# Feed-forward's first rows and weight pieces prepared in the second attention's last batch

## The reference, cut to what matters

```python
x = x + tanh(g_xattn[0]) * L0_xattn(layernorm(x), ctx)
x = x + tanh(g_ffn[0])   * L0_experts(layernorm(x))
x = x + tanh(g_xattn[1]) * L1_xattn(layernorm(x), ctx)     # "second attention", 16 heads of 32, 256 + 16 keys
x = x + tanh(g_ffn[1])   * L1_ffn(layernorm(x))

def L1_ffn(x):                                             # 512 -> 2048 -> 512
    h = gelu(x @ proj1.T + proj1_bias)                     # exact gelu
    return h @ proj2.T + proj2_bias
```

## Time and profile before

| | us |
|---|---|
| median of three runs | 3754.83 |
| lowest and highest | 3752.32, 3757.24 |
| the profiled execution | 3753.35 |
| its span on the core | 3751.6 |
| TensorE busy | 3583.4 (96%) |
| VectorE busy | 2179.9 (58%) |
| ScalarE busy | 1822.8 (49%) |
| GpSimd busy | 1532.9 (41%) |
| attention, first instruction to first of the feed-forward | 2243.5 to 2988.9 |
| feed-forward | 2988.9 to 3751.6 |

### The profile page before, as it was taken

How to read it: one execution, slowest core, us unless ns; L and a number is a source line. 1 busy time by engine, 2 the same in 40 slices (tenths; PEclk the granted TensorE clock), 3 DMA queues, 4 the chain that set the end, 5 groups by cost and what they waited for, 6 DMA issues and landing times. The chain is left out here.

```text
span 3751.6 us, 68000 instructions
## 1 busy us (share of the span) xinstructions
PE 3583.4 (96%) x23268; PEld 3105.6 (83%) x23268; DVE 2179.9 (58%) x5409; ACT 1822.8 (49%) x4696; POOL 1532.9 (41%) x1536
## 2 busy tenths in 40 slices
PE   7999999999999997799999987999999699999999
PEld 7999999999999996799999975666666478877887
DVE  6666666556666665567666776777777352222221
ACT  4444454544444443455555535777777442222222
POOL 3333333534444444456655645666776330000000
PEclk9999999999999998899999998999999799999999
DMA  4566665315666651666666652222121120000000
GB/s 151 178 222 228 229 217 210 125 67 213 220 216 220 220 207 57 241 236 237 238 229 235 237 183 79 60 65 65 61 69 36 55 79 23 23 23 23 23 23 23
DMA packets 228534, 520.22 MB, mean 139 GB/s; under 512 B 12289, under 2 KB 29058, under 8 KB 224242
## 3 DMA queue, kind: packets, MB, share of 16 engines
q1 hardware_dynamic: 123634, 296.43, 22.8%
q10 hardware_dynamic: 94432, 187.71, 13.6%
q0 software_dynamic: 10272, 33.63, 2.7%
HBM read 266.58 MB, written 251.13 MB: 138 GB/s over the span
## 5 line engine op out<-in xcount | busy, mean ns | idle before, releaser
L672 POOL TENSOR_SCALAR a_prob<-a_prob,a_rinv 128x256 f32<-128x256 f32 x512 | 471.3, 932 | 835.9 <-DVE a_rinv L855 835.9
L619 ACT ACTIVATE a_prob<-a_prob,a_low_bias 128x256 f32<-128x256 f32 x512 | 256.5, 502 | 458.7 <-DVE a_low_bias L846 458.7
L2209 DVE TENSOR_TENSOR f_h_lo<-f_h_f,f_h_hi 128x512 fp32r<-128x512 f32 x128 | 104.0, 813 | 456.4 <-ACT f_h_hi L2166 456.4
L1122 PE MATMUL e_gb<-e_xt_hi,in_hi 128*128 128x256 f32 x1248 | 355.0, 284 | 5.7 <-DVE e_xt_lo L1248 5.7
L1123 PE MATMUL e_gb<-e_xt_lo,in_hi 128*128 128x256 f32 x1248 | 354.8, 284 | 0.0
L1124 PE MATMUL e_gb<-e_xt_hi,in_lo 128*128 128x256 f32 x1248 | 354.7, 284 | 0.0
L1106 POOL TENSOR_TENSOR e_act_hi<-e_act_f,e_zeros 128x256 fp32r<-128x256 f32 x156 | 235.2, 1508 | 285.2 <-DVE e_act_f L1268 273.6
L2164 ACT ACTIVATE f_h_f<-f_hb,f_b_sb 128x512 f32<-128x512 f32 x128 | 88.0, 688 | 477.3 <-PE f_hb L2090 417.8
L422 PE MATMUL a_pj<-a_xt,a_wq_hi 128*128 128x256 f32 x1024 | 310.2, 303 | 0.9 <-DVE a_q_lo L705 0.9
L424 PE MATMUL a_pj<-a_xt,a_wq_lo 128*128 128x256 f32 x1024 | 289.4, 283 | 0.0
L423 PE MATMUL a_pj<-a_xt,a_wq_hi 128*128 128x256 f32 x1024 | 289.1, 282 | 0.0
(11 more groups left out here) (311 smaller groups left out, 11463.7 us busy)
## 6 DMA issues: line engine op xcount, KB each, us to landing
w_raw<-in_w_gate SPq DMA_DIRECT2D x39, 2048.0 KB, 7.9
x_sorted<-a_blank ACTq DMA_DIRECT2D x42, 1792.0 KB, 6.5
y_sorted<-a_blank ACTq DMA_DIRECT2D x42, 1792.0 KB, 8.7
w_raw<-in_w_out SPq DMA_DIRECT2D x39, 1024.0 KB, 5.0
e_xg<-x_sorted SPq DMA_DIRECT2D x39, 512.0 KB, 8.5
y_sorted<-e_y_sb SPq DMA_DIRECT2D x39, 512.0 KB, 2.8
xt_rows<-a_xt SPq DMA_DIRECT2D x16, 1024.0 KB, 5.1
a_xt<-xt_rows SPq DMA_DIRECT2D x16, 1024.0 KB, 6.2
```

The source lines that it names most:

```text
L619: e = nc.scalar.activation(prob[:, u % 4, t], prob[:, u % 4, t], ACT.Exp, bias=low_bias[:, u % 2, t:t + 1], scale=-1.0, accum_out=rsum[:, ...
L672: p = nc.gpsimd.tensor_scalar(prob[:, u % 4, t], prob[:, u % 4, t], rinv[:, u % 2, t:t + 1], None, ALU.mult)
L1122: nc.tensor.matmul(out, a_hi, b_hi, start=start, stop=False)
```

## The change

Part of what `first` did is moved into the last steps of the attention, and the results are left in buffers that live on:

- `w_raw` becomes `raw_in` and `raw_out`. `raw_in`, `in_hi`, `in_lo`, `dca_hi`, `dca_lo`, the identity, b1 and the feed-forward's gate are kept over both stages; `raw_out` ends with the attention. The class `Ahead` names the places: the first rows and the normalised rows in the two halves of `nrm`, pieces 0 and 1 in the places of the attention's `wd` and `wkv`, the transposed rows' high and low part in the place of `wq`. Piece 2 goes over `wo` later.
- SP, behind all loads of the attention: piece 0 into `y_sb`, rows 0 to 511 into `raw_in`, piece 1 into `x2`; b1 and the gate among the constants at the attention's start.
- In the last batch, counted in steps from the last pair (`past`): ACT casts half a piece at the end of steps -9, -8, -5, -4, and two transposed column blocks at the end of steps 0 and 1. DVE makes low parts in steps -8, -7, -4, -3, statistics in -6 and -5, the normalised rows in -2, low parts of the transposed rows in 1 and 2. POOL has the root in -4. PE transposes 8 blocks in step 0 and 8 in step 1, into the score banks; the low and high parts then come from there. Groups 0 and 1 of `last_out` move from step 2 to step 0.
- The feed-forward begins with `hidden(0, 0, 0)`. SP loads piece 2, piece 3, rows 512 to 1023, b2. DVE multiplies b2 by the gate behind the low part of step 1 and adds it to the first rows in step 12. All low parts from piece 2 on are GpSimd's, as before.

```diff
+class Ahead:
+    def __init__(self, b1, gate, first, b1_sb, gate_t, raw_in, in_hi, in_lo):
+        self.x_first, self.xn = raw_in[:, 1, :, 0:D], raw_in[:, 1, :, D:2 * D]
+        self.first_hi, self.first_lo = ([w[:, 1, n:n + 2].rearrange("p a (b d) -> p (a b) d", b=2) for n in (2, 0)] for w in (in_hi, in_lo))
+        self.xt_hi, self.xt_lo = in_hi[:, 0, :, 0:D], in_lo[:, 0, :, 0:D]
...
 # attention, sync
+            sp.wait_ge(y_used, B)
+            sp.dma_start(ff_raw[0], ahead.first[0]).then_inc(ff_loaded[0], 16)
+            sp.wait_ge(ready["qk"], GROUPS * (B - 1))
+            for bb in range(2):
+                sp.wait_ge(x_stored[bb], 64)
+            sp.dma_start(ahead.x_first, x_out[0:2 * S, :].rearrange("(t p) d -> p t d", p=P)).then_inc(ff_x_loaded, 16)
+            sp.wait_ge(x_used, B)
+            sp.dma_start(ff_raw[1], ahead.first[1]).then_inc(ff_loaded[1], 16)
 # attention, tensor
+            def turn_ahead(m):
+                pe.wait_ge(ff_xn, 1)
+                pe.wait_ge(e_done, B * PAIRS + m + 1)
+                for j in range(2):
+                    c = 2 * m + j
+                    for t in range(4):
+                        mm = nc.tensor.transpose(sc[:, m, j, t * P:(t + 1) * P], ahead.xn[:, t, c * P:(c + 1) * P], ident[:])
+                    mm.then_inc(ff_turned, 1)
...
+                if past == 0:
+                    turn_ahead(0)
                 if pair(i, u - 2):
                     turn_p(i, u - 2, 0)
+                if past == 0:
+                    last_out(i, (u - 2) // PAIRS, "o0", [0, 1])
+                if past == 1:
+                    turn_ahead(1)
                 if past == 2:
-                    last_out(i, u // PAIRS - 1, "o0", list(range(GROUPS - 1)))
+                    last_out(i, u // PAIRS - 1, "o0", [2])
...
+                if past == 0:
+                    last_out(i, (u - 2) // PAIRS, "o1", [0, 1])
                 if past == 2:
-                    last_out(i, u // PAIRS - 1, "o1", list(range(GROUPS - 1)))
+                    last_out(i, u // PAIRS - 1, "o1", [2])
 # attention, scalar
+            def split_ahead(n, half):
+                rows = slice(2 * half, 2 * half + 2)
+                act.wait_ge(ff_loaded[n], 16)
+                act.wait_ge(ready["v0"], B)
+                nc.scalar.copy(ahead.first_hi[n][:, rows], ff_raw[n][:, rows]).then_inc(ff_hid, 1)
...
+                past = LOOP * i + u - (B * PAIRS - 1)
+                if past in (-9, -8):
+                    split_ahead(0, past + 9)
+                if past in (-5, -4):
+                    split_ahead(1, past + 5)
+                if past in (0, 1):
+                    for c in range(2 * past, 2 * past + 2):
+                        turned_ahead(c)
 # attention, vector
+                if past in (-8, -7):
+                    low_ahead(0, past + 8)
+                if past in (-6, -5):
+                    normalize_ahead(past + 6)
+                if past in (-4, -3):
+                    low_ahead(1, past + 4)
+                if past == -2:
+                    normalize_ahead(2)
+                if past in (1, 2):
+                    for c in range(2 * past - 2, 2 * past):
+                        turned_low_ahead(c)
 # feed_forward
-            load_rows(0, 0)
-            load(0)
-            sp.dma_start(ident[:], identity).then_inc(id_loaded, 16)
-            load(1)
...
+            load(2)
             load(3)
             load_rows(1, 1)
-            sp.wait_ge(t_ready, FC)
-            load(2)
+            sp.dma_start(b2_sb[:], b2).then_inc(b_loaded, 16)
...
-            def first():
-                for c in range(FC):
-                    turn(0, c)
-                low_done(pe, 0)
-                hidden(0, 0, 0)
+            hidden(0, 0, 0)
```

More of the change, by code:

```diff
@@ L1904, in take, with low_ahead, normalize_ahead, turned_low_ahead @@
                 op.then_inc(taken[use], 1)
+            def low_ahead(n, half):
+                rows = slice(2 * half, 2 * half + 2)
+                dve.wait_ge(ff_hid, 2 * n + half + 1)
+                low(ahead.first_lo[n][:, rows], ff_raw[n][:, rows], ahead.first_hi[n][:, rows]).then_inc(ff_lod, 1)
+            def normalize_ahead(part):
+                x = ahead.x_first
+                if part == 0:
+                    dve.wait_ge(ff_x_loaded, 16)
+                    for t in range(4):
+                        l = V.bn_stats(ff_stats[:, t], x[:, t])
+                    l.then_inc(ff_stat, 1)
+                elif part == 1:
+                    dve.wait_ge(ff_stat, 1)
+                    dve.nop(nofuse=True)
+                    for t in range(4):
+                        l = V.bn_aggr(ff_mv[:, t], ff_stats[:, t])
+                    l.then_inc(ff_stat, 1)
+                    dve.wait_ge(ff_stat, 2)
+                    V.tensor_scalar(ff_var[:], ff_mv[:, :, 1], LN_EPS, None, ALU.add).then_inc(ff_stat, 1)
+                else:
+                    dve.wait_ge(ff_root, 1)
+                    dve.wait_ge(ready["qk"], GROUPS * B)
+                    for t in range(4):
+                        l = V.tensor_scalar(ahead.xn[:, t], x[:, t], ff_mv[:, t, 0:1], ff_rstd[:, t:t + 1], ALU.subtract, ALU.mult)
+                    l.then_inc(ff_xn, 1)
+            def turned_low_ahead(c):
+                dve.wait_ge(ff_xt_hid, c + 1)
+                low(ahead.xt_lo[:, c], sc[:, c // 2, c % 2], ahead.xt_hi[:, c]).then_inc(ff_lod, 1)
             def step(i, u):
@@ L2041, in feed_forward, with all_chunks @@
         LINKS = 4
-        def all_chunks(eng, first, chunk):
-            first()
+        def all_chunks(eng, chunk):
             for b in range(2):
@@ L2137, in chunk @@
                         turn(n + 1, TURN[j])
-            all_chunks(pe, first, chunk)
+            all_chunks(pe, chunk)
         @block.scalar
@@ L2143, in split @@
             def split(n):
-                act.wait_ge(w_loaded[n % 4], 16 * (n // 4 + 1))
-                nc.scalar.copy(pieces[n][1], raw(n)).then_inc(w_hid, 1)
+                act.wait_ge(w_loaded[n % 4], 16 * ((n - 2) // 4 + 1))
+                nc.scalar.copy(w_hi[n], raw(n)).then_inc(w_hid, 1)
             def turned(n, b, c):
-                act.wait_ge(t_ready, FC * n + c + 1)
-                nc.scalar.copy(xt_hi[:, b, c], tb[c % 2][:]).then_inc(xt_hid, 1)
-            def first():
-                split(0)
-                act.wait_ge(c_loaded, 16 * len(consts))
-                nc.scalar.activation(gate_t[:], gate_t[:], ACT.Tanh).then_inc(gate_done, 1)
-                split(1)
-                for c in range(FC):
-                    turned(0, 0, c)
+                act.wait_ge(t_ready, FC * (n - 1) + c + 1)
+                nc.scalar.copy(xt_hi[b][:, c], tb[c % 2][:]).then_inc(xt_hid, 1)
             def chunk(i, b, last, is_first=False):
@@ L2198, in chunk @@
                 if is_first:
-                    for n in range(4, len(pieces)):
+                    for n in range(4, PIECES):
                         split(n)
-            all_chunks(pool, lambda: root(0), chunk)
+            all_chunks(pool, chunk)
         @block.vector
@@ L2246, in turned, with first_bias, first_sum @@
             def turned(n, b, c):
[L2247 to L2263 removed]
+                dve.wait_ge(xt_hid, FC * (n - 1) + c + 1)
+                low(xt_lo[b][:, c], tb[c % 2][:], xt_hi[b][:, c]).then_inc(xt_lod, 1)
+            def first_bias():
+                dve.wait_ge(b_loaded, 16)
+                V.tensor_scalar(b2_sb[:], b2_sb[:], gate_t, None, ALU.mult).then_inc(bias_done, 1)
+            def first_sum():
                 dve.wait_ge(bias_done, 1)
[L2265 removed]
+                for t in range(TC):
+                    l = V.tensor_tensor(x_sb[0][:, t], x_sb[0][:, t], b2_sb[:], ALU.add)
+                l.then_inc(bias_done, 1)
             def chunk(i, b, last, is_first=False):
```

184 lines of the change are left out of this document (92 added, 92 removed).

## The result

| | before | after |
|---|---|---|
| median, us | 3754.83 | 3731.69 |
| lowest and highest | 3751.82, 3757.24 | 3726.12, 3734.68 |
| profiled execution, us | 3753.35 | 3731.69 |
| its span | 3751.6 | 3729.9 |
| TensorE busy | 3583.4 | 3581.6 |

The ratio of after to before is 0.9939, 95% interval 0.9924 to 0.9953. The medians differ by 23.1 us, the two profiled executions by 21.7. So the traces have 21.7 us to explain, against a forecast sum of 20.3.

What follows compares the result with a forecast made beforehand. The prediction took TensorE to bound the feed-forward, idle before it behind a 20 us latency chain. Terms -20.5 + 0 + 0.8 + 0 + 1.2 - 1.8 = -20.3 from 3753.35, plus 1.5, gave 3734.6 us; range 3727.5 to 3742.

Steps and rivals of the forecast that it cites:

- The feed-forward's start: TensorE's first feed-forward matmul starts 0.3 us after the stage opens, at 2989.2 in place of 3009.7: -20.5 us.
- Piece 2 and the pieces behind it: Weight loads at the feed-forward's start keep up with the earlier first matmul: 0, at most +2 us.
- the row of the same position: Piece 2, now the stage's first load, lands in 5.7 us like the load formerly in that place, so nothing waits: 0.
- The clock at the feed-forward's start: First feed-forward matmuls run at half speed for about 4.6 us, 1.5 us more than before: +0.8 us, range -0.5 to +0.8.
- The bias step: VectorE's b2 times gate, between low parts 1 and 2, waits for GpSimd's split, still just in time: 0, at most +0.5.
- The last batch: In the attention's last batch, two ScalarE half splits before short waits delay the chain by 0.66 + 0.54: +1.2 us.
- The attention's end: Output matmuls moved forward save 4.1 us; they and new transposes cost 1.2 and 1.1 back: -1.8 us, the least certain term.
- The variant at 2.4 GHz throughout: Full TensorE clock over the end of the attention: -5.3 us in place of -1.8, time 3731.1, within the forecast's 0.62.
- Rival (a): Transposes and moved matmuls at the end of the attention run at 1.2 GHz: +2.3 us, time 3738.7, chance 0.22.
- (b): First rows' load, or pieces 3 to 5, come late and half the gain goes: 3744.6 us, chance 0.09.
- (c): Last batch is one chain of latencies, so all moved work, 32.9 us, is paid there: 3768.0 us, chance 0.04.
- (d): First feed-forward matmul still waits for something of its stage, so no gain: 3756 us with the batch's costs, chance 0.03.

Runs made afterwards that it cites:

- turn_in_ff_2: Changed kernel with the 16 transposes of the first rows and their splits back at the feed-forward's start, piece 2 loaded behind them: 3738.3 us, ratio 0.9959.
- warm_2: Changed kernel with 16 matmuls of no use behind TensorE's last output matmul, before the feed-forward opens: 3729.2 us, ratio 0.9939.
- piece_third_2: Changed kernel with the feed-forward's first loads reordered: rows of the second chunk, weight piece 3, then piece 2, which is used first: 3737.1 us.
- outs_back: Changed kernel with the 12 output matmuls put back two steps later, the 16 transposes staying ahead: 3731.9 us, 0.9929 to 0.9956 of before.
- again: The changed kernel run once more with no edit: 3732.3 us, ratio 0.994 to the kernel before.
- splits_shift: Changed kernel with two ScalarE half splits moved from short waits to longer ones in the last batch, VectorE's low parts one step later: 3731.6 us.
- no_prep_2: Changed kernel without the new ScalarE, VectorE and GpSimd work in the last batch, so part of the computation is missing: 3730.4 us, 0.992 to 0.9947 of before.

## Why the prediction was right, point by point

**The feed-forward's start** (-20.5): -20.44. The 0.3 us taken from the entry into the attention was measured as 0.31. turn_in_ff_2 checks the last part of the chain alone, 6.2 us against 6.3.

**Piece 2 and the pieces behind it** (0, up to +2): 0. ScalarE doesn't wait for piece 2, and for piece 4 it waits 2.46 us, as it did before (2.51). The forecast took 5.7 us for the landing; warm_2 has 5.0, against 7.1 us at which ScalarE is ready. That the order of the loads carries this term, piece_third_2 shows: the row of the same position was the right one to take.

**The clock at the feed-forward's start** (+0.8): the matmuls run at 1.2 GHz for 5.2 us, against 3.1 before, so +1.05; the forecast had 4.6 us. How long it lasts differs between executions of the same order of work: from the first matmul on the granted clock stays at 0.50 for 5.5 us here, for 3.4 in outs_back and for 6.0 in again. From the first matmul to the end it takes 1.85 us longer. Besides the clock's part, TensorE's waits for low parts in the first chunk are 0.31 and 0.15 us where before there was one of 0.22, and the seven later waits for low parts are 6.7 us against 6.0 in all. This last 0.7 us was in no term of the forecast. The seven waits are 6.5 to 7.1 us in all ten traces with the changed feed-forward and 6.0 in all four without it, so it comes with the change; why is open, since no edit here was aimed at it. warm_2 shows the cause of the clock's part: the idle time ahead.

**The bias step** (0): 0, and by the mechanism that was written down. The step ran 4.83 us, to the end of GpSimd's split, and low part 2 was in time by 0.35 us. I didn't take the step out in a run; the rows are the whole evidence.

**The last batch** (+1.2): +1.45 in the two traces. The rows of ScalarE look as described, with 1.10 us a half split in place of 0.95 and the copies behind still waiting 0.29 and 0.32. But splits_shift and no_prep_2 say that reading the term so was more exact than the batch allows: the agreement of 1.45 with 1.2 is partly luck. The delay of a step can be given back by the next ones. That TensorE, at a clock of 0.50 to 0.84, is what is late in those is likely but wasn't isolated. The term is between 0 and 1.5 us.

**The attention's end** (-1.8): -4.96. This is the mis-sized term. The step of the prediction that failed is its choice of clock, "I take the value between that comes with the clock as the rows have it". The rows had 1.2 GHz, but that clock belonged to the waits which the change fills. The variant at 2.4 GHz throughout, -5.3, was within 0.4 of the result. The prediction put the variant in its range but argued from the clock of before. The Trainium skill (TensorE: Matmul & The Clock Gate, section "A second HAM failure mode: psum-queue depth-cycling", just behind the one that the prediction names) tells of a kernel in which short idle times between groups of matmuls come often enough that the clock goes back and forth between its two levels. The trace agrees: with waits of 0.7 to 1.0 us before it the clock fell, to 0.50 and 0.63 in the two halves of 2970 to 2980, and with the waits filled it is 1.00. Rival (a), the end at the lower clock, is ruled out: all ten traces of the changed kernel and its variants have 1.00 from 2970 to 2980. Within the term, the move of the matmuls is worth 1.3 us and the 16 transposes cost 0.5, both at 2.4 GHz; that leaves some 4.2 of the 5 us for the clock, an estimate from these traces.

**The rivals.** (b), late data: no wait for the first rows or pieces appears in the last batch, and what ends TensorE's 0.54 us of idle time ahead of the new transposes is the exponentials, not data. (c), a serial last batch: no_prep_2 has it within 0.2 us of the same length. (d), nothing starts earlier: no.

Together: -20.44 + 1.85 + 1.45 - 4.96 = -22.1, and 0.4 of another sign ahead of the last batch, which is scatter between executions: -21.7. Two errors partly cancelled, 3.2 us too little gain at the attention's end and 1 too little cost in the feed-forward. That the sum came within 1.4 us is in that part luck; that it stood on the term of -20.5 is not.

## What to carry to other kernels

Where a stage begins with a chain of latencies and the stage ahead ends with waits, the chain can be moved whole: count the gap on the critical engine, and look for the first input that must still be loaded. A clock read from the rows of before holds for the old order of work only; where an edit fills TensorE's waits, work the term out at 2.4 GHz as the main case. And where the granted clock lies under 1.00 on a path, idle TensorE time is the thing to fill, with useful work or, as here, with 43 matmuls of no use that brought 3731.7 us (0.9939 of before) down to 3723.0 (0.9914).

## What the runs showed of the hardware that was not expected

Adding work of no use to the critical engine shortened a stretch of the trace three times: 16 transposes theirs from 19.3 and 20.3 to 15.6 us, 16 matmuls ahead of a barrier the part behind it by 2.0 us (at a price of 0.6 ahead of it), and 27 in the last batch that batch from 58.1 to 49.2 us; the last is the one that the program's time shows clearly. The clock fell behind waits of 1.0 us and less. A VectorE instruction that took 0.48 us by itself took 4.83 beside GpSimd's split of 5.07, and the next one on its chain was still in time by 0.35 us. And the last batch of one and the same program took between 56.6 and 58.5 us from one execution to the next, its clock changing at other moments each time; differences of a microsecond in such a stretch can't be read from single traces.
